# Expert layers of a hybrid block on one core: three of four batches computed per routed line instead of per expert

## What is computed

```python
logits = jnp.einsum('btd,ed->bte', x, router_w)      # 8 experts
top_vals, top_idx = jax.lax.top_k(logits, 2)
top_w = jax.nn.softmax(top_vals, axis=-1)
h = jnp.square(jax.nn.relu(jnp.einsum('nd,edh->enh', xf, w1)))   # 128 -> 256
y = jnp.einsum('enh,ehd->end', h, w2)                            # 256 -> 128
y_sel = y[idx_f, jnp.arange(N)[:, None]]             # only two of the eight are used
out = jnp.einsum('nk,nkd->nd', w_f, y_sel)
```

## Time and profile before

| | us |
|---|---|
| median of 3 runs (lowest, highest) | 1291.15 (1289.55, 1291.58) |
| the profiled execution's own time | 1293.22 |
| its span in the trace | 1291.4 |
| layer 2, from its first router product to the first maximum | 91.2 to 323.6 |
| the sixteen steps ahead of the first group | 323.6 to 367.2 |
| attention, steps from 0 on | 367.2 to about 1069 |
| layer 4 and the last store | 1069 to 1291.4 |

### The profile page before, as it was taken

One profiled execution on the slowest core, in us unless ns is written; L12 is line 12 of the kernel. 1 busy time (PEld: TensorE's weight loads), 2 busy tenths in 40 slices (PEclk: granted clock), 3 DMA queues, 4 the chain that ended last, 5 costly groups with the idle time before them and its releaser, 6 DMA issues.

```text
span 1291.4 us, 25944 instructions
## 1 busy us (share of the span) xinstructions
PE 1201.4 (93%) x10003; PEld 737.2 (57%) x10003; DVE 1060.5 (82%) x2485; ACT 906.3 (70%) x1714; POOL 287.3 (22%) x328
## 2 busy tenths in 40 slices
PE   1779999998889999999999999999999999999998
PEld 0368999887434434444444444444444348899998
DVE  7668888887888898989898888988889816787886
ACT  1046556655158898888898888988888995656564
POOL 2032000003423333333332333332322100000000
PEclk9679999999569999999999999999999999999999
DMA  5100000000000000000000000000000000000000
GB/s 192 36 1 1 1 1 1 2 1 2 0 1 2 2 1 2 2 1 2 1 2 1 1 2 1 2 1 2 1 2 2 1 2 1 10 17 9 10 9 17
DMA packets 6137, 11.10 MB, mean 9 GB/s; under 512 B 1907, under 2 KB 3574, under 8 KB 5878
## 3 DMA queue, kind: packets, MB, share of 16 engines
q1 hardware_dynamic: 6014, 9.45, 2.2%
HBM read 7.28 MB, written 2.10 MB: 7 GB/s over the span
## 4 chain that ended last, share of the span: by engine, by line
PE 78%; DVE 13%; ACT 5%; issue 3%; DMA 1%; SPq 0%; DVEq 0%; ACTq 0%
PE acc L1296 17%; PE six L1127 17%; PE six L1267 10%; DVE mxp L960 8%; PE six L1116 6%; PE six L1118 6%; PE six L1117 6%; PE misc L1267 5%; ACT PB L653 3%; PE six L1280 2%; PE six L1233 1%; ACT SC L642 1%; PE six L1228 1%; DVE nt L670 1%; PE misc L1116 1%
## 5 line engine op out<-in xcount | busy, mean ns | idle before, releaser
L960 DVE TENSOR_REDUCE mxp<-six 128x2 f32<-128x1024 f32 x512 | 598.8, 1218 | 75.6 <-PE six L1280 73.6
L653 ACT ACTIVATE PB<-six 128x512 f32<-128x512 f32 x681 | 384.8, 599 | 60.8 <-PE six L1267 36.9
L1296 PE MATMUL acc<-PB,Vg 128*32 128x256 f32 x4096 | 328.2, 393 | 16.3 <-ACT SC L642 16.3
L1280 PE MATMUL six<-K,Q 32*128 32x512 f32 x1024 | 264.1, 519 | 14.5 <-DVE mxp L960 10.0
L1267 PE MATMUL six<-Q,K 32*128 32x512 f32 x681 | 272.2, 498 | 0.1
L1127 PEld LDWEIGHTS six<-w2s,PB 128*128 128x128 f32 x2048 | 246.9, 192 | 9.3
L1127 PE MATMUL six<-w2s,PB 128*128 128x128 f32 x2048 | 250.6, 276 | 0.0
L550 ACT ACTIVATE PB<-six 128x512 f32<-128x512 f32 x256 | 151.5, 599 | 141.1 <-PE six L1118 124.8
L653 ACT ACTIVATE PB<-misc 128x512 f32<-128x512 f32 x343 | 205.4, 599 | 23.2 <-PE six L1267 16.8
L1267 PEld LDWEIGHTS six<-Q,K 32*128 32x128 f32 x681 | 107.9, 183 | 143.0 <-ACT PB L653 74.5
L858 DVE SCALAR_TENSOR_TENSOR x<-six,wexp,x 128x128 f32<-128x128 f32 x512 | 143.8, 343 | 40.0 <-PE six L1127 38.3
(11 more groups left out here) (235 smaller groups left out, 1146.4 us busy)
## 6 DMA issues: line engine op xcount, KB each, us to landing
x<-in_x SPq DMA_DIRECT2D x4, 512.0 KB, 5.7
SC<-in_w_om SPq DMA_DIRECT2D x1, 2048.0 KB, 14.3
out<-x SPq DMA_DIRECT2D x8, 256.0 KB, 2.0
VH<-in_w SPq DMA_DIRECT2D x1, 1024.0 KB, 9.4
Vg<-in_wqs SPq DMA_DIRECT2D x1, 256.0 KB, 7.3
Vg<-in_wks SPq DMA_DIRECT2D x1, 256.0 KB, 6.6
cst<-in_cst SPq DMA_DIRECT2D x1, 81.5 KB, 3.5
nwb<-in_nw SPq DMA_DIRECT2D x1, 64.0 KB
```

Of the source, the lines that this page charges most:

```text
L653: act.activation(PB[:, s % 3, j, :], scores, ACT.Exp).then_inc(G_("act_taken"), 1)
L960: dve.reduce_max(dst, taken_slot("max", s, i).rearrange("p (a n) -> p a n", a=2), AX.X).then_inc(G_("max_taken"), 1)
L1280: ins = pe.matmul(slot[:, c * BLK:(c + 1) * BLK], Q[rows, G % NG, t * P:(t + 1) * P], K[rows, G % NG, th * BLK:(th + 1) * BLK], start=True ...
L1296: ins = pe.matmul(acc[RB * j:RB * (j + 1), n], Vg[:, G % 2, t, j, :], PB[:, s % 3, j, n], start=(t == 0 and half == 0), stop=(t == TPB - 1 ...
```

## The change

Batch 0 of each expert layer stays as it was, two blocks through all experts. Batches 1 to 3 go by place. While the dense blocks run, batches 1 and 2 are normalised a whole batch at a time, routed, and each line gets two places, one in the range of each of its experts, where the ranges are rounded up to tiles of 128 lines: at most 23 tiles (`RT`). POOL sends the lines there with 16 indirect DMAs for a batch (128 lines each) into a buffer in memory, SP loads the 23 tiles back and loads each tile's own 128x256 slice of the first weights by an expert number that it reads into a register, PE turns each tile, multiplies it in plain fp32 (no high and low parts) by these weights, and by second weights in SBUF whose address it reads into a register as well. SP keeps the results in a second buffer in memory, POOL fetches them back with another 16 indirect DMAs for a batch, and DVE adds them to x with their weights. Batch 3 is routed while batch 1 is computed.

Other edits: both squares of a dense expert go to ACT; the router is one plain fp32 product for each 128 lines, so its split weights, ACT's copy and the transposes go; the first weights get a buffer of their own (`w1s`), which later holds two of the three weight slots; five of the attention's statistics (blocks 2 to 6) move from layer 2 into the attention's steps; the first projections move beside batches 2 and 3; POOL fills `MX` with zeros later; the end of the attention uses the bank `acc` instead of `misc`; the two buffers for lines are filled with zeros once (three DMAs of 1.5 MB).

The core of the diff:

```diff
+SPARSE = range(1, B)
+SEND = 2 * TPB
+RT = (2 * L + E * (P - 1)) // P
+TG = 4
+RGROUPS = -(-RT // TG)
+PAIRS = -(-RT // 2)
...
@@ SP @@
+            def load_lines(f, b):
+                n = sparse_index(f, b)
+                sp.wait_ge(G_(f"sent{b}"), 16 * SEND * (f + 1))
...
+            def load_weights(f, b, g):
+                n = RGROUPS * sparse_index(f, b) + g
+                sp.wait_ge(G_("te_ready"), sparse_index(f, b) + 1)
+                if n >= 3:
+                    sp.wait_ge(G_("hidp_done"), pair_count(n - 3))
+                for r in range(TG * g, min(RT, TG * (g + 1))):
+                    e = sp.value_load(te[0:1, b, r:r + 1], min_val=0, max_val=E - 1)
+                    sp.dma_start(weights_slot(n)[:, r % TG * HID:(r % TG + 1) * HID],
+                                 a["w1"][ds(e, 1)].rearrange("o d h -> (o d) h")).then_inc(G_(f"line{g}"), 16)
...
+            for f in range(2):
+                load_lines(f, 1)
+                if f:
+                    for u in range(2):
+                        sp.wait_ge(G_("comb_done"), E * (2 + u + 1))
+                        store(0, u)
+                for m in range(3):
+                    load_weights(f, 1, m)
+                for m in range(RGROUPS * len(SPARSE)):
+                    b, g = m // RGROUPS + 1, m % RGROUPS
+                    if g == RGROUPS - 3 and b + 1 < B:
+                        load_lines(f, b + 1)
+                    if m + 3 < RGROUPS * len(SPARSE):
+                        load_weights(f, (m + 3) // RGROUPS + 1, (m + 3) % RGROUPS)
+                    keep_lines(f, b, g)
...
@@ POOL @@
+            def send(f, b):
...
+                pl.wait_ge(G_("dest_ready"), n + 1)
+                for i in range(TPB):
+                    for k in range(2):
+                        pl.indirect_dma_start(xs[b], bass.IndirectOffsetOnAxis(ap=dest[:, b, k, i:i + 1], axis=0),
+                                              hbs[:, b % 2, i, :], None).then_inc(G_(f"sent{b}"), 16)
+            def fetch(f, b, i):
+                for k in range(2):
+                    pl.indirect_dma_start(lines_back[b][:, k, i, :], None, yd[b],
+                                          bass.IndirectOffsetOnAxis(ap=dest[:, b, k, i:i + 1], axis=0)
+                                          ).then_inc(G_(f"back{b}{i // TPK}"), 16)
...
-            for n in range(2, NBLK):
-                low_part(1, n)
+            for b in SPARSE:
+                send(0, b)
...
             low_part(2, 0)
-            split_out(0, 0)
             low_part(2, 1)
-            for t in range(1, 4):
+            for t in range(4):
                 split_out(0, t)
+            fetch_batch(0, 1)
+            fetch_batch(0, 2)
             pl.wait_ge(*act_taken("v", 1))
...
                     split_out(G + 2, 0)
+                if b == 0:
+                    if g == 0:
+                        wait_kept(pl, 0, 3)
+                    fetch(0, 3, 2 * g)
+                    fetch(0, 3, 2 * g + 1)
...
-            for n in range(1, NBLK):
-                low_part(3, n)
+            low_part(3, 1)
+            for b in SPARSE:
+                send(1, b)
+            for b in SPARSE:
+                fetch_batch(1, b)
...
@@ ACT, steps of the attention @@
+                if s == 0:
+                    act.wait_ge(G_("mixed"), 2 * sparse_index(0, 2) + 2)
+                    wait_kept(act, 0, 3)
...
@@ DVE @@
+            def sparse_beside(f, b, q):
+                if b == 1:
+                    if q in (0, 1):
+                        link(rows_stats(3, q))
+                    elif q == 2:
+                        rows_scale()
+                    elif q in (4, 5):
+                        rows_apply(f, 3, q - 4)
+                    elif q == 9:
+                        batch_top_two(f, 3)
+                    elif q == 10:
+                        batch_weights(f, 3)
+                    elif q == 11:
+                        batch_places(f, 3)
...
+                elif b == 3 and q in (10, 11):
+                    add_results(f, 1, q - 10)
...
+                for b in SPARSE:
+                    for q in range(PAIRS):
+                        relu_pair(f, b, q)
+                        sparse_beside(f, b, q)
...
+                if G < 0 and kk in (9, 10):
+                    add_results(0, 2, kk - 9)
+                if G in (4, 5) and kk == 4:
+                    add_results(0, 3, G - 4)
+                if (G, kk) in late_stats:
+                    attention_stats(late_stats[G, kk])
+                if (G, kk - 2) in late_stats:
+                    attention_rsqrt(late_stats[G, kk - 2])
...
             experts(1)
+            for b in (2, 3):
+                for u in range(2):
+                    add_results(1, b, u)
...
@@ PE @@
+            def turn_lines(f, b, g):
+                n = RGROUPS * sparse_index(f, b) + g
+                pe.wait_ge(G_("tw_ready"), sparse_index(f, b) + 1)
+                pe.wait_ge(G_(f"line{g}"), line_count(f, b, g))
...
+                for i in range(min(TG, RT - TG * g)):
+                    r = TG * g + i
+                    expert_at[b, r] = pe.value_load(tw[0:1, b, r:r + 1], min_val=0, max_val=CH * D * (E - 1))
+                    ins = pe.transpose(line_bank(n)[:, i * P:(i + 1) * P], lines_in[b][:, r, :], ident)
+                ins.then_inc(G_("lines_turned"), 1)
+            def lines_hidden(f, b, q):
...
+                for r in range(2 * q, min(RT, 2 * q + 2)):
+                    lines = hTs[:, group % 2, r % TG * P:(r % TG + 1) * P]
+                    for c in range(CH):
+                        at = (r % 2 * CH + c) * P
+                        ins = pe.matmul(big[:, n % 2, at:at + P], tile_weights(group, r % TG, c), lines,
+                                        start=True, stop=True)
+                ins.then_inc(G_("hidp_done"), 1)
+            def lines_result(f, b, q):
...
+                        ins = pe.matmul(big[:, 2 + group % 2, r % TG * D:(r % TG + 1) * D], sqs[:, n % 3, at:at + P],
+                                        w2f[:, ds(expert_at[b, r] + c * D, D)],
+                                        start=(c == 0), stop=(c == CH - 1))
```

587 lines of the change are left out of this document (453 added, 134 removed).

## The result

The changed kernel takes 1418.9 us (median of 4 runs, 1417.5 to 1419.8) where the kernel before took 1290.4 beside it (1289.6 to 1291.6): a ratio of 1.099, 95% interval 1.098 to 1.100. It is 128.5 us slower. I had forecast 1272, some 19 us faster, with a range from 1212 to 1340.

The account below looks back on a forecast made before the run. PE was taken to bound the expert layers and DVE the gap between them. Layer 2 -27, attention +9 and layer 4 -1 gave -19 us on the profiled 1293.2, a median of 1272 us, range 1212 to 1340.

Parts of the forecast that it names:

- 1.65 us a tile: Expert tiles on PE: 0.77 issuing, 0.7 register read, 0.18 waits and address sums; 114 us a layer.
- rival 4: Tiles: register reads hide in PE's queue, a tile takes 1.15 us, total 1207 us; chance 0.20.
- SP. ... about 1.4 us, below 1.65 ... Both hide, narrowly: Tiles: SP's read, issue, keeping and line loads take about 1.4 us a tile; these and the weight load hide beside PE.
- signs of being wrong: Pair under 2.5 or over 3.8 us, half clock in tiles, dense block over 40 us, or PE waiting mid-batch for weights or lines.
- Rival 2: Tiles: the clock falls to half, nine instructions take 1.92 us, 37 us more, 1309 us; chance 0.12.
- My third for PE's work in the steps ahead of the attention: Steps between layer 2 and attention: PE's work at full speed was a third of the 43.6 us, yet the clock fell to 0.50.
- Rival 1: Tiles: register reads of 1.15 us stall PE, a tile takes 2.1 us, 62 us more, 1334 us; chance 0.25.
- Rival 3: POOL and DVE block each other: an indirect DMA takes 2 us, uncovered sets cost 26 us more, 1298 us; chance 0.08.
- Two engines at 30 and 31 us with waits between them: I take 34 us: Four remaining dense blocks: DVE 30 and PE 31 us, so 34 us a block, 68 for two; bounds 31 and 40.
- The 8 steps that hold it ... cost 1.3 us: Attention: one norm job costs 1.3 us, from 22.4 us against 21.1 for eight steps; five moved jobs cost 6.5 us.
- End of layer 2: POOL's first fetch stands behind the last split_out, DVE waits 19 us for it plus 2 to land; layer ends at 200.
- Layer 4's hole and tail: Layer 4: PE idles 7 us before the tiles; an uncovered 19 us fetch, landing, additions and store follow them.

Follow-up runs that it names:

- g2: The change with SP's register read ahead of each weight load replaced by a fixed expert; 22 us shorter than the change.
- f1: The change with both register reads constant (fixed experts) and each group's results stored one group later; 1323.0 us, ratio 1.020 to the kernel before.
- g1: The change with PE's register read ahead of each turn replaced by a fixed expert; 44 us shorter than the change.
- g3: The change with a group's results stored one group later on SP, behind the next weights; 45 us shorter than the change.
- f3: The change without register reads or norm jobs in attention, with later storing, later dense-block routing and batch 1 fetched before the splits; 1270.0 us, ratio 0.979 to before.
- g8: The change, whole computation kept, with later storing, dense-block routing one expert step later and batch 1 fetched before the splits; 1341.1 us, 3.0% over before.
- e4: The change with the six norm jobs left out of the attention steps (stale statistics), kernel before beside it; 1509.1 us.
- the first set: Eight runs of edited forms of the change with only the kernel before beside them; 1457.2 to 1525.6 us.
- e1: The change with PE's register read replaced by a constant (fixed experts), in the first set; 1501.3 us.

## Why the prediction was wrong

**The tile.** The read was sized well, though I had it as a guess between two bounds: 0.66 us between turns that wait for it, where I took 0.7. The rule of the Trainium skill that I set beside it ("DMA: Bandwidth & Descriptors", section "Latency and other measured facts": a floor of about 600 ns) is close to it: the 0.66 holds the turn besides the read, and on SP a read adds 0.61 us (issues of weights stand 1.10 us apart in the change and 0.49 in g2). As an estimate it would have taken the forecast further from the result. Without a wait in front the work of a group took less than my 1.65 us a tile: from 251.24 to 255.86 are 4.6 us for four tiles, the reads hidden, which is rival 4's mechanism; over a whole stretch even f1 had 1.5 us a tile (102.0 / 69).

The step that failed is "**SP. ... about 1.4 us, below 1.65 ... Both hide, narrowly**". I compared throughputs of two engines. The change ties them in a ring: SP loads a group's weights (one every 1.10 us, as I had priced them with 1.12), 2.1 us pass to the landing, PE turns and multiplies, ACT stores the result, and only then does SP pass its wait for that result, behind which the next loads stand. Latencies of a ring add where throughputs hide. g1, g2 and g3 show it: each part shortens the whole, by 44, 22 and 45 us. What stands behind the wait of keep_lines on SP I had not asked, and it is worth the 45 us of g3. Of my signs of being wrong three came: PE waited in mid-batch for weights, a pair took 4.2 to 4.5 us where I had drawn the line at 3.8, and a dense block took over 40. Whether PE gains by waiting for a group's weights at its products instead of at its turn wasn't tried.

**The clock.** Rival 2 gave it to the tiles, and it was part of the truth: the granted clock is 0.80 in the tiles, not 0.5, and a pair's eight instructions take 1.06 us at 2.4 GHz and 1.91 to 1.94 at 1.2. By the order in the rows it is a consequence: the slow rows stand behind gaps of some 4 us, the second group above has neither, and f1, which took three causes of waiting away, has 0.90 and 0.88. (My third for PE's work in the steps ahead of the attention was read too low: 35.8 us busy at half clock are 17.9 at full speed, 0.41 of 43.6.) It also falls in the dense blocks and the attention, where I hadn't looked for it.

**Rival 1** had the sign and nearly the number (2.1 us a tile; measured 145.0/69 = 2.1 and 156.1/69 = 2.3), for a wrong reason: not a read of 1.15 us, but one of 0.66 plus SP's ring. With the 77 us that the other stages missed its 1334 would be 1411.

**Rival 3** fell: an indirect DMA took 0.96 us of POOL and 0.30 to the next (16 in 20 us, forecast 19), and none of the 192 over 1.17, beside a busy DVE too. The Trainium skill's rule on the shared port ("SBUF — State Buffer", "SBUF: two separate sides") is not refuted by that, as most of DVE's work there reads PSUM; no run tried it. What the trace does show is the block on DVE's side, in the attention below.

**Dense blocks.** The step "Two engines at 30 and 31 us with waits between them: I take 34 us" failed; it took 42 to 47, above my bound of 40. PE waits for the routing's rows and rank:

```profile
150.32 1.11 PE L1546 MATMUL misc<-cst,hbs 128*128 128x128 f32 x4 [5.10 <-DVE hbs L1187]
...
152.08 0.63 PE L1498 MATMUL six<-hTl,w1h 128*128 128x512 f32 x1
152.51 0.63 PE L1496 MATMUL six<-hTh,w1h 128*128 128x512 f32 x1
...
166.06 0.43 PE L1564 MATMUL six<-both,tri 128*128 128x64 f32 x2 [1.46 <-DVE both L1207]
166.33 1.68 PE L1566 MATMUL six<-both,ones 128*128 128x56 f32 x14
167.86 3.40 PE L1569 MATMUL six<-both,ones 128*128 128x8 f32 x16
```

5.10 us of waiting for DVE, then products 0.43 us apart instead of 0.23, and the 32 instructions of the rank take 5.1 us (166.06 to 171.1), the last 16 of them 0.20 us apart at the lower clock, where I had 0.085 us each. One expert step more of lead gave 12.5 and 6.3 us back (f3 against f1; g8 against g3: 11.6 and 5.0), which shows the wait as part of the cause. The remaining 78.0 us, and 85.2 with layer 4's hole, are still above the forecast of 68 and 75, and what holds them wasn't tried.

**Attention.** "The 8 steps that hold it ... cost 1.3 us" failed. ACT's store of the accumulator ends every 8 steps:

```profile
427.52 0.60 ACT L880 ACTIVATE SC<-acc 128x512 f32<-128x512 f32 x1
456.65 0.60 ACT L880 ACTIVATE SC<-acc 128x512 f32<-128x512 f32 x1
478.71 0.60 ACT L880 ACTIVATE SC<-acc 128x512 f32<-128x512 f32 x1
```

From store to store, the same eight steps in three kernels (us; 2 is the stretch that ends with the second store). J is a norm job of the change, A an addition of batch 3; the kernel before has its one job in 7 and 8. All other stretches agree within 0.1 us, but for the first (28.9, 29.8 with a job, 29.2 without).

```
stretch             2 J   4 J   6 J    8    9 A  11 A  14 J  16 J
before             22.1  22.1  21.1  23.4  23.2  22.1  21.1  22.3
the change         29.1  29.2  26.2  22.2  25.9  25.3  25.1  23.5
f3 (no jobs)       22.1  22.1  21.2  22.2  28.5  29.2  21.2  22.2
```

So a job cost 7.1, 7.0, 5.1, 4.0, 1.2 and, in the first stretch, 0.9 us: 25 in all, less the 1.2 of the job that left stretch 8, where I had 6.5. The two additions cost 5.9, where I had 2.7. Together that is the 21 us that I missed. I had also read the 1.3 us off the wrong neighbours: stretch 7, the 22.4 us of the earlier trace rows, takes 22.4 in the change too, without a job. The job of before showed in stretch 8 (23.4 against 22.2), and that my number was near it is luck.

In the stretches of 29.1 us the granted clock is 0.82, in the next 1.00: PE waits for DVE's maxima, and behind the waits its rows are slow. DVE's own work grew there by 5.9 us (19.3 to 25.2), and in stretches 6, 14 and 16 by 2.8, 2.7 and 2.5. Most of the difference is two instructions of the job: they last 1.2 us beside POOL's work on two operands and end with it to 0.02 us, where they last 0.16 in stretch 16. It is what the earlier trace rows showed, and rival 3's mechanism on the side of DVE.

```profile
432.97 1.18 DVE L912 SCALAR_TENSOR_TENSOR nt<-nt,ve 128x4 f32<-128x4 f32 x1
434.19 1.20 DVE L913 SCALAR_TENSOR_TENSOR rs<-nt,rs 128x4 f32<-128x4 f32 x1
...
432.86 1.27 POOL L561 TENSOR_TENSOR hTl<-VH,hTh 128x512 fp32r<-128x512 f32 x1 [5.08 <-ACT hTh L701]
434.09 1.28 POOL L589 TENSOR_TENSOR x<-x,cbb 128x512 f32<-128x512 f32 x1
```

No run moved a job by a step or two to keep it clear of POOL, so how much of the 7 us this is stays open, as does why a job costs 5 us in stretch 6 and 1.2 in stretch 16. Without the six jobs the attention lost 21.7 us (f3 against f1), 3.6 a job; e4 had said 27 to 33. That is less than the sum above, because the additions cost more once the jobs are gone (5.3 and 7.1 us).

**End of layer 2.** The mechanism was as forecast:

```profile
327.13 1.01 POOL L543 DMA_INDIRECT SC<-yd,dest  x1 [0.15 <-issue]
...
338.52 2.31 DVE L1249 SCALAR_TENSOR_TENSOR x<-SC,pw,x 128x128 f32<-128x128 f32 x8 [11.39 <-DMA SC<-yd,dest]
348.53 2.31 DVE L1249 SCALAR_TENSOR_TENSOR x<-SC,pw,x 128x128 f32<-128x128 f32 x8 [7.37 <-DMA SC<-yd,dest]
```

I let the fetch begin 12 us ahead of PE's end; in the trace it begins 0.7 us behind the last full pair's rectification, since the splits came late. Fetching first shortens the end of the layer from 24.3 to 5.7 us (f1, f3; 24.3 to 5.8 from g3 to g8), and the tiles get up to 5.4 us longer by it (102.0 to 107.4; 128.0 to 128.8 from g3 to g8): 13 to 18 us in all, more than the 8 that this term had missed.

**Layer 4's hole and tail** were right: 9.0 us for 7, and 33 for 30. The tail rests on 1.2 us for an indirect DMA, the middle of two bounds, and it measured 1.25: a lucky middle.

```profile
1221.76 8.33 SPq L468 DMA_DIRECT2D w1s<-in_w  x8
...
1387.84 0.95 POOL L543 DMA_INDIRECT hbs<-yd,dest  x1 [18.66 <-DMA yd<-PB]
...
1399.14 2.31 DVE L1249 SCALAR_TENSOR_TENSOR x<-hbs,pw,x 128x128 f32<-128x128 f32 x8 [10.06 <-DMA hbs<-yd,dest]
```

**What stays open:** how much of a wait's price is the clock behind it (no run took the one without the other), and why four forms of the change took 106 to 134 us longer in the first set, and the kernel before hardly (1292.6 and 1293.8 us).

## What to carry to other kernels

When a change makes two engines feed each other with few buffers between, walk once round the ring (issue, landing, product, store, the wait in front of the next issue) and add the latencies; comparing each engine's throughput isn't enough, and an in-order queue must not wait for a result ahead of loads that are already possible. Work saved on a full engine can be paid for again where it then waits: here the granted clock fell from near 1.0 to 0.8 in the stretches with waits. When a stage loses time in a few steps, compare it step by step with the same steps of before; a neighbour can differ for reasons of its own. A set of experiments needs the changed kernel itself beside it, not only the kernel before.

## What the runs showed of the hardware that I had not expected

- PE's register reads hide when products are queued ahead (four turns together at 251.24) and cost 0.66 us each, with the turn, when they are not; without a read four turns take 0.63 us.
- Cutting a 128 KB load to 8 KB with the same number of issues changed the median by 3 us in 1420.
- Two small DVE instructions took 1.18 and 1.20 us instead of 0.16 while POOL worked on two operands, and the eight steps around them 29.1 us instead of 22.1; none of 192 indirect DMAs on POOL took over 1.17 us.
- On two chips four kernels ran 106 to 134 us longer than the same kernels on a third, most of it in the stretches with dense transfers (tiles of e1 166.8 and 189.7 us, of g1 135.8 and 135.2), with gaps of 1.5 to 2.4 us between single products and at one place SP's four issues nearly twice as long (6.76 us for 3.65). The page lists instruction queues among the DMA queues; that the supply of instructions was held up is only a guess.
